# Leaf rows of two trees added on VectorE before the transpose, the low part of x on POOL, and one semaphore signal for each pair of halves

## The chip, the cores and the metric

The kernel runs on one core of a Trainium2 chip. The metric is the device time of one execution in microseconds (us). The program works through 32 units (pairs of images) in a software pipeline: three unrolled bodies fill it, a hardware loop runs over units 2 to 29, three unrolled bodies drain it.

## The reference, cut to what matters

```python
h = patchify(x) @ W.T + b                       # 64 images, 196 tokens, 768 -> 256
n = layernorm(h)
xn = n / max(norm(n) / 16, eps) * g
uv = silu(xn @ uv_w.T)                          # u (512), v (512), base (128)
q, k = rope(base * gamma + beta)
a = u * (square(relu((q @ k.T + w_rel) / sqrt(128))) @ v)
h = h + (n * res_scale + a @ o_w.T)
y = layernorm(h)                                # fast feed-forward: 8 trees of depth 7
logits = y @ W_in.T + b_in                      # 8 trees x 255 nodes
walk = root, then left or right by the sign of the node's logit, 7 times
out = h + (silu(logits) * on_the_walk) @ W_out.T
```

Only the 8 nodes on a token's walk through each tree contribute. In trees 0 to 3 the kernel treats the leaf apart: it fetches one row of a table in DRAM for each token (input weights, bias, output weights of the leaf that the walk ends in), forms the leaf's logit as a dot product, and adds `silu(logit) * output row`.

## The kernel before, in words

All large products run in float32 as three matmuls (`product`, lines 1140 to 1144): a value is split into a high part (rounded, made on ScalarE by `high`) and a low part (value minus high part, a subtraction on VectorE by `low`, line 835). A product is `hi*lo + lo*hi + hi*hi`. A unit has 392 tokens, held as 4 groups of 98.

One body of the pipeline works on up to four units at once: `p`, `i`, `n`, `nx` follow each other, `nx` is being loaded and embedded, `n` is in layer norm and attention, `i` and `p` are in the trees. Each engine has its own hand-written list of steps, `body(p, i, n, nx)`, and executes it in that order; semaphores tie the lists together. The steps that matter here:

- Embedding: ScalarE `x_high(n, k)`, VectorE `x_low(n, k)`, TensorE `embed(n, k)` for six chunks k in a ring of three buffers. `embed` signals `x_used` after every chunk.
- First layer norm: `turn_h(n, 0, m)` transposes h on TensorE in two halves m, VectorE `norm_stats` and `norm_moments`, POOL `norm_roots` (a power, a product, a product), ScalarE `norm_apply` and `make_xn`, TensorE `turn_xn` in two halves, ScalarE `xn_high`, VectorE `xn_low`, TensorE `turn_normed` in two halves, VectorE `residual(n, 0)` and `(n, 1)`, TensorE `make_base`, ScalarE `silu_base`, TensorE `make_v`. `make_base` waits for `residual(n, 0)`, since both use bank 0 of `front`; `make_v(n, 1)` writes that bank again and waits for `silu_base`.
- Trees: `tree_logits(i, t, b)` (b counts halves of 128 nodes), VectorE `decisions`, TensorE `tree_visits`, ScalarE `silu_tree`, VectorE `mask`, ScalarE `hid_high`, VectorE `hid_low`, TensorE `tree_out(i, t, m)` into `out_acc`, VectorE `final`, then the store.
- Leaves of trees s = 0 to 3: TensorE `find_leaf(i, s)`, ScalarE `leaf_number`, POOL `fetch_rows(i, s, g)` (one indirect DMA for each group g), VectorE `leaf_dots(i, s)`, ScalarE `leaf_silu` and `scale_rows(i, s)` (four products of 98x256), TensorE `add_rows(i, s)`: eight transposes that add the scaled rows into `out_acc` (line 1378). The rows lie in eight slots, so that two trees are held at a time; `fetch_rows(i, s, 0)` waits until `add_rows` of two trees before has freed the slots.

POOL otherwise makes the low parts of late weights (`split_late`, line 445), in the first two bodies only.

Of the kernel before, what the change touches and what calls it, by code (L numbers as in the profile page):

```python
# [24 lines left out]
ALU = mybir.AluOpType  # L25
# [19 lines left out]
DC = D // P  # L45
# [10 lines left out]
XRING = 3  # L56
UV = 2 * E + S
# [5 lines left out]
ROW_IN, ROW = D + 1, 2 * D + 1  # L63
ROW_SLOTS = 8
# [51 lines left out]
def vit_tower(nc, x, cols, tok_w, uv_w, o_w, in_w, out_w, rel, rope, anc, ident_in, out):  # L116
    ctx = ExitStack()
    with ctx:
# [121 lines left out]
        rows_added, held_ok = sem("rows_added"), sem("held_ok")  # L240
# [195 lines left out]
        def _(pool):  # L436
# [9 lines left out]

            def norm_roots(n, which):
# [13 lines left out]
            def fetch_rows(i, s, g):  # L461
# [3 lines left out]
                if g == 0:  # L465
# [3 lines left out]
                    if GROUPS * (s + 1) > ROW_SLOTS or not first(i):  # L469
                        pool.wait_ge(rows_added, GATHERED * i + s + 1 - ROW_SLOTS // GROUPS)  # L470
# [15 lines left out]
            def body(p, i, n, nx):  # L486
# [6 lines left out]
                fetch_rows(i, 1, 0)  # L493
                late_splits(i, n, 2)
                fetch_rows(i, 1, 1)
# [8 lines left out]
                late_splits(i, n, 4)  # L504
                fetch_rows(i, 3, 1)
                fetch_rows(i, 3, 2)
                fetch_rows(i, 3, 3)
                norm_roots(n, 1)
                norm_roots(nx, 0)
# [16 lines left out]
        def _(act):  # L526
# [3 lines left out]
            def x_high(n, k):  # L530
# [3 lines left out]
                if k >= XRING or not first(n):  # L534
                    act.wait_ge(x_used, n * XC + k - XRING + 1)
# [5 lines left out]
            def copy_h(n, m):  # L541
# [3 lines left out]
                if m == 0:  # L545
                    act.wait_ge(x_used, n * XC + XC)
# [48 lines left out]
            def scale_base(n, which):  # L595
# [3 lines left out]
                if which == 1:  # L599
                    act.wait_ge(normed_turned, 2 * n + 2)  # L600
# [47 lines left out]
            def ffn_x_high(n, m):  # L648
                if n is None:
                    return  # L650
                act.wait_ge(ffn_x_turned, 2 * n + m + 1)
                if m == 0 and not first(n):
                    act.wait_ge(logits_ready, HALVES * n)
# [12 lines left out]
            def silu_tree(i, t, b):  # L666
# [5 lines left out]
                if b == 1:  # L672
                    act.wait_ge(logits_ready, HALVES * i + halves_before(t + 1))
# [12 lines left out]
            def hid_high(i, t):  # L686
# [3 lines left out]
                if t >= 2 or not first(i):  # L690
                    act.wait_ge(tree_added, 2 * (TREES * i + t - 1))
# [38 lines left out]
            def body(p, i, n, nx):  # L730
                silu_tree(p, 7, 1)
# [3 lines left out]
                silu_tree(p, 7, 0)  # L735
                copy_h(n, 1)
                scale_rows(p, 3)
                hid_high(p, 7)
                silu_tree(i, 0, 0)
                hid_high(i, 0)  # L740
                silu_tree(i, 1, 0)
                norm_apply(n, 0, 0)
                norm_apply(n, 0, 1)
                norm_apply(n, 0, 2)
                leaf_number(i, 0)
                silu_tree(i, 2, 0)
# [4 lines left out]
                make_xn(n, 3)  # L751
                leaf_number(i, 1)
# [3 lines left out]
                leaf_number(i, 2)  # L756
                hid_high(i, 2)
                silu_tree(i, 3, 0)
                x_high(nx, 0)
                silu_base(n)  # L760
                scale_base(n, 1)
                scale_base(n, 0)
                leaf_silu(i, 0)
                silu_v(n, 0)
# [802 lines left out]
```

## Time and profile before

| | |
|---|---|
| median of 3 runs | 2202.95 us (2196.44 to 2209.55) |
| the profiled execution | 2201.36 us |
| its span, first to last instruction | 2199.5 us |
| TensorE matmul busy | 2066.1 us (94%) |
| VectorE busy | 1621.5 us (74%) |
| ScalarE busy | 1395.2 us (63%) |
| POOL busy | 774.1 us (35%) |

Busy times count an engine's own instructions. Matmuls overlap in the array and their ends are modelled, so 94% is not the share of what the array could do; the pitch from one start to the next is the better measure. Idle time of an engine costs something only where another waits for it, in the end TensorE.

### The profile page before, as it was taken

The page shows a single profiled execution, that of the slowest core. Times are in us where ns is not written, and L with a number is a line of the kernel's source. Part 1 is how long each engine was busy: PE and PEld are TensorE (multiplying, and loading weights), DVE is VectorE, ACT ScalarE, POOL GpSimd, SP SyncE. Part 2 cuts the span into 40 slices and gives each one's busy share as a digit, 9 for nine tenths or more (in the row PEclk, how much of TensorE's full clock was granted, in tenths as well). Part 3 has the DMA queues.
Part 4 walks back from the last instruction along what each step waited for, and adds up shares of the span by engine and source line. Part 5 has one row for each costly group of instructions (what it writes and reads, how often), then busy time and mean ns, then how long its engine had stood idle before and what let it go on. Part 6 is the DMA issues. An engine that isn't in the chain of part 4 may idle for free.

```text
span 2199.5 us, 42461 instructions
## 1 busy us (share of the span) xinstructions
PE 2066.1 (94%) x13256; PEld 1941.8 (88%) x13256; DVE 1621.5 (74%) x4210; ACT 1395.2 (63%) x3085; POOL 774.1 (35%) x905
## 2 busy tenths in 40 slices
PE   6899999999999999999999999999999999999997
PEld 5789889899988898888998898988889988889887
DVE  5678777777777787777777777777777877777775
ACT  5556666666666566566666665666665666656654
POOL 2752333232333333332323333323323233333233
PEclk8999999999999999999999999999999999999999
DMA  5331322222322223222223222222223232222222
GB/s 146 85 94 52 89 73 66 73 76 63 83 71 65 81 55 84 75 64 73 77 62 84 70 73 73 64 75 77 65 70 84 55 85 69 73 73 66 63 67 74
DMA packets 81999, 163.13 MB, mean 74 GB/s; under 512 B 17102, under 2 KB 48048, under 8 KB 81968
## 3 DMA queue, kind: packets, MB, share of 16 engines
q0 software_dynamic: 40960, 103.02, 17.4%
q1 hardware_dynamic: 41008, 59.71, 9.3%
q8 instruction: 17, 0.28, 0.1%
q14 instruction: 14, 0.11, 0.0%
HBM read 148.76 MB, written 13.90 MB: 74 GB/s over the span
## 4 chain that ended last, share of the span: by engine, by line
PE 84%; another core or an unknown queue 5%; ACT 4%; POOL 3%; issue 2%; DVE 1%; DMA 1%; ACTq 0%; POOLq 0%; SPq 0%; DVEq 0%
PE front L1142 10%; PE front L1144 9%; PE front L1143 9%; PE hid_ps L1142 9%; PE hid_ps L1143 9%; PE hid_ps L1144 9%; PE out_acc L1142 6%; PE out_acc L1143 6%; PE out_acc L1144 6%; PE out_acc L1378 4%; PE front L1177 2%; PE front L1184 2%; PE hid_ps L1366 2%; PE hid_ps L1337 2%
## 5 line engine op out<-in xcount | busy, mean ns | idle before, releaser
L474 POOL DMA_INDIRECT leaf_rows<-leaf_table,leaf_at x512 | 532.4, 1040 | 163.9 <-issue 163.4
L453 POOL TENSOR_TENSOR inv_root<-to_root,minus_half 98x8 f32<-98x8 f32 x64 | 111.0, 1734 | 728.3 <-DVE to_root L885 404.6
L528 ACT ACTIVATE hid_hi<-hid 128x392 fp32r<-128x392 f32 (+1 forms) x256 | 177.8, 695 | 237.1 <-PE out_acc L1144 155.4
L1142 PE MATMUL out_acc<-hid_hi,outw_lo 128*128 128x392 f32 x768 | 293.4, 382 | 2.6 <-DVE hid_lo L835 2.3
L1142 PE MATMUL hid_ps<-ffn_x,in_lo 128*128 128x392 f32 x768 | 282.3, 368 | 6.2 <-POOL in_lo L445 5.8
L1143 PE MATMUL hid_ps<-ffn_x,in_hi 128*128 128x392 f32 x768 | 266.3, 347 | 0.0
L1144 PE MATMUL hid_ps<-ffn_x,in_hi 128*128 128x392 f32 x768 | 264.7, 345 | 0.0
L1144 PE MATMUL out_acc<-hid_hi,outw_hi 128*128 128x392 f32 x768 | 264.6, 345 | 0.0
L1143 PE MATMUL out_acc<-hid_lo,outw_hi 128*128 128x392 f32 x768 | 264.4, 344 | 0.0
L473 POOL TENSOR_TENSOR held<-minus_half 98x1 f32<-98x1 f32 x128 | 47.2, 369 | 489.9 <-issue 428.7
L718 ACT ACTIVATE leaf_rows<-leaf_rows,leaf_act 98x256 f32<-98x256 f32 x512 | 218.2, 508 | 0.1
L996 DVE SCALAR_TENSOR_TENSOR hid<-hid_ps,hid 128x392 f32<-128x392 f32 x384 | 203.1, 557 | 11.7 <-PE hid_ps L1337 11.3
L835 DVE TENSOR_TENSOR hid_lo<-hid,hid_hi 128x392 fp32r<-128x392 f32 (+1 forms) x256 | 196.0, 766 | 13.8 <-ACT hid_hi L528 9.4
L1015 DVE CUSTOM_DVE_ANT_0 leaf_rows<-leaf_rows,leaf_x 98x257 f32<-98x257 f32 x512 | 188.2, 421 | 16.8 <-DMA leaf_rows<-leaf_table,leaf_at 16.4
L980 DVE TENSOR_SCALAR decide<-hid_ps,col 128x392 bf16<-128x392 f32 x256 | 156.4, 620 | 38.6 <-PE hid_ps L1144 35.5
L683 ACT ACTIVATE hid<-hid_ps,col 128x392 f32<-128x392 f32 x256 | 150.9, 590 | 38.1 <-DVE decide L980 38.1
L1142 PE MATMUL front<-uv_hi,xn 128*98 128x512 f32 x256 | 110.4, 431 | 51.1 <-ACT bases L593 43.3
L1142 PEld LDWEIGHTS hid_ps<-ffn_x,in_lo 128*128 128x128 f32 x768 | 149.6, 195 | 7.1 <-POOL in_lo L445 6.4
L1142 PE MATMUL front<-xn,uv_lo 128*128 128x392 f32 x320 | 113.9, 356 | 43.6 <-issue 42.2
L1142 PEld LDWEIGHTS out_acc<-hid_hi,outw_lo 128*128 128x128 f32 x768 | 147.2, 192 | 8.6 <-DVE hid_lo L835 3.0
L1143 PEld LDWEIGHTS out_acc<-hid_lo,outw_hi 128*128 128x128 f32 x768 | 147.6, 192 | 3.2
L1143 PEld LDWEIGHTS hid_ps<-ffn_x,in_hi 128*128 128x128 f32 x768 | 148.2, 193 | 0.0
(140 smaller groups left out, 5808.2 us busy)
## 6 DMA issues: line engine op xcount, KB each, us to landing
x_raw<-x SPq DMA_DIRECT2D x192, 196.0 KB, 2.4
out<-out_stage SPq DMA_DIRECT2D x32, 392.0 KB
leaf_rows<-leaf_table,leaf_at POOLq DMA_INDIRECT x512
leaf_table<-leaf_rows SPq DMA_DIRECT2D x4, 256.5 KB, 4.7
out_stage<-in_w SPq DMA_DIRECT2D x4, 256.0 KB
tok_major<-tok_w SPq DMA_DIRECT2D x3, 256.0 KB, 4.3
late_raw<-out_w SPq DMA_DIRECT2D x6, 128.0 KB
u<-uv_w SPq DMA_DIRECT2D x1, 576.0 KB, 4.2
```

Source lines behind the costliest of these rows:

```text
L453: pool.tensor_tensor(inv_root[:, 0:size], to_root[:, 0:size], minus_half[:, 0:size], ALU.pow).then_inc(roots_ok, 1)
L474: pool.indirect_dma_start(row_slot(s, g), None, table, bass.IndirectOffsetOnAxis(ap=leaf_at[:, s, g:g + 1], axis=0), element_offset=s * P ...
L528: act.activation(out, src, ACT.Copy).then_inc(done, 1)
L683: act.activation(hid_t[:, t % 2, b], hid_ps[:, t % 2, b, 0:T], ACT.Silu, bias=bias).then_inc(activated, 1)
L718: act.activation(w, w, ACT.Copy, scale=leaf_act[:, s, g:g + 1]).then_inc(rows_scaled, 1)
L835: dve.tensor_tensor(out, src, hi.bitcast(F32), ALU.subtract).then_inc(done, 1)
L980: dve.tensor_scalar(decide[:, t % 2], hid_ps[:, t % 2, 0, 0:T], c(COL_B_IN + 2 * t), 0.0, ALU.add, ALU.is_gt).then_inc(decided, 1)
L996: dve.scalar_tensor_tensor(hid_t[:, t % 2, b], hid_ps[:, t % 2, 1, 0:T], VISITED[b], hid_t[:, t % 2, b], ALU.is_ge, ALU.mult).then_inc(mas ...
L1015: dve.tensor_tensor_reduce(w, w, normed2[:, g], 1.0, 0.0, ALU.mult, ALU.add, leaf_logit[:, s, g:g + 1]).then_inc(dotted, 1)
L1142: pe.matmul(out, w[1], x_parts[0], start=start, stop=False)
L1143: pe.matmul(out, w[0], x_parts[1], start=False, stop=False)
L1144: return pe.matmul(out, w[0], x_parts[0], start=False, stop=stop)
```

## The change

1. Leaf rows. ScalarE scales the rows of trees 0 and 2 only. VectorE has a new step, `merge_rows(i, s)` for s = 1 and 3: `row(s) * leaf_act(s) + row(s - 1)`, four instructions. `add_rows` is called for s = 1 and 3 alone and turns the sum. The slots of trees 0 and 2 are free once the merge is done (`rows_merged`), those of 1 and 3 after `add_rows`.
2. The low part of x is made on POOL (`x_low`) from the second unit on, VectorE keeps it for the first (`first_x_low`).
3. One signal for a pair of halves: `x_used` after chunks 2 and 5 only, `h_turned`, `xn_turned`, `normed_turned`, `ffn_x_turned`, `tree_added` after the second half, `logits_ready` after a tree's last half. The waits follow.
4. The lists of TensorE, VectorE and ScalarE are written in another order, and the bodies of TensorE, VectorE and ScalarE are cut at another place (TensorE's now begins with `tree_out(p, 0, 0)`).

```diff
+X_SIGNALS = (2, 5)
+COUPLES = GATHERED // 2
 # POOL
+            def x_low(n, k):
+                if n is None or first(n):
+                    return
+                if k == 0 and isinstance(n, int) and n == 1:
+                    pool.wait_ge(x_lo_ok, XC)
+                pool.wait_ge(x_hi_ok, n * XC + k + 1)
+                pool.tensor_tensor(x_lo[:, k % XRING], x_raw[:, k % XRING], x_hi[:, k % XRING].bitcast(F32),
+                                   ALU.subtract).then_inc(x_lo_ok, 1)
...
-                        pool.wait_ge(rows_added, GATHERED * i + s + 1 - ROW_SLOTS // GROUPS)
+                        couple = COUPLES * i + (s // 2 + 1 - ROW_SLOTS // GROUPS // 2)
+                        if s % 2 == 0:
+                            pool.wait_ge(rows_merged, GROUPS * couple)
+                        else:
+                            pool.wait_ge(rows_added, couple)
 # ScalarE
-                    act.wait_ge(x_used, n * XC + k - XRING + 1)
+                    act.wait_ge(x_used, 2 * n + k // XRING)
...
-                act.wait_ge(xn_turned, 2 * n + m + 1)
+                act.wait_ge(xn_turned, n + 1)
 # VectorE
+            def merge_rows(i, s):
+
+                if i is None:
+                    return
+                dve.wait_ge(leaf_active, GATHERED * i + s + 1)
+                dve.wait_ge(rows_scaled, GROUPS * (COUPLES * i + s // 2 + 1))
+                for g in range(GROUPS):
+                    one, two = (row_slot(n, g)[:, ROW_IN:ROW] for n in (s - 1, s))
+                    dve.scalar_tensor_tensor(two, two, leaf_act[:, s, g:g + 1], one,
+                                             ALU.mult, ALU.add).then_inc(rows_merged, 1)
...
-                dve.wait_ge(normed_turned, 2 * n + m + 1)
+                dve.wait_ge(normed_turned, n + 1)
...
-                dve.wait_ge(logits_ready, HALVES * i + halves_before(t) + 1)
+                dve.wait_ge(logits_ready, TREES * i + t + 1)
 # TensorE
-                last.then_inc(x_used, 1)
+                if k in X_SIGNALS:
+                    last.then_inc(x_used, 1)
...
-                last.then_inc(done, 1)
+                if m == DC - 1:
+                    last.then_inc(done, 1)
...
-                last.then_inc(logits_ready, 1)
+                if b == halves(t) - 1:
+                    last.then_inc(logits_ready, 1)
...
-                last.then_inc(tree_added, 1)
+                if m == DC - 1:
+                    last.then_inc(tree_added, 1)
...
-                pe.wait_ge(rows_scaled, GROUPS * (GATHERED * i + s + 1))
+                pe.wait_ge(rows_merged, GROUPS * (COUPLES * i + s // 2 + 1))
```

Where instructions now stand. First TensorE in the loop, from the transposes of `xn` to the second product for v (`tok_major` holds the normalised rows, `front<-xn,uv_lo` begins `make_base`, `front<-uv_hi,xn` is `make_v`, `out_acc` is `tree_out`, `leaf_steps` is `find_leaf`, `toward` is `tree_visits`). Before:

```order
L1184 MATMUL front<-ident,tok_major 128x98 [waits xn_tm_ok]
...
L1366 MATMUL hid_ps<-leaf_steps,taken 98x1 [waits masked,taken_ok]
...
L1184 MATMUL front<-ident,tok_major 128x98 [waits xn_lo_ok]
L1184 MATMUL front<-ident,tok_major 128x98 x3
L1142 MATMUL out_acc<-hid_hi,outw_lo 128x392 [waits hid_lo_ok]
...
L1337 MATMUL hid_ps<-decide,toward 128x392 [waits leaf_at_ok,masked,decided]
L1142 MATMUL front<-xn,uv_lo 128x392 [waits res_added]
...
L1142 MATMUL hid_ps<-ffn_x,in_lo 128x392 [waits leaf_at_ok,masked]
...
L1142 MATMUL front<-uv_hi,xn 98x512 [waits res_added]
...
L1142 MATMUL front<-uv_hi,xn 98x512 [waits base_ok]
```

Now:

```order
L1218 MATMUL front<-ident,tok_major 128x98 [waits xn_tm_ok]
...
L1403 MATMUL hid_ps<-leaf_steps,taken 98x1 [waits masked,taken_ok]
...
L1515 COMPARE_AND_BRANCH
L1174 MATMUL out_acc<-hid_hi,outw_lo 128x392 [waits hid_lo_ok,out_ready]
...
L1218 MATMUL front<-ident,tok_major 128x98 [waits xn_lo_ok]
L1218 MATMUL front<-ident,tok_major 128x98 x3
...
L1174 MATMUL out_acc<-hid_hi,outw_lo 128x392 [waits hid_lo_ok]
...
L1174 MATMUL front<-xn,uv_lo 128x392 [waits res_added]
...
L1174 MATMUL front<-uv_hi,xn 98x512 [waits res_added]
L1175 MATMUL front<-uv_lo,xn 98x512
L1176 MATMUL front<-uv_hi,xn 98x512
...
L1174 MATMUL front<-uv_hi,xn 98x512 [waits base_ok]
```

Both halves of `turn_normed` now stand together, two pieces of `tree_out` (six matmuls) stand between them and `make_base`, and one more piece stands between the two products for v. `tree_visits(i, 3)` and `tree_logits(i, 4, 0)` have moved ahead of the first `turn_normed`, and the loop's branch lies in this stretch.

Next POOL in the loop, from the last fetches of a body to its end. Before:

```order
L473 TENSOR_TENSOR held<-minus_half 98x1 [waits held_ok,rows_added,leaf_at_ok]
L474 DMA leaf_rows<-leaf_table,leaf_at 98x513 x4
L453 TENSOR_TENSOR inv_root<-to_root,minus_half 98x4 [waits moments_ok]
L456 TENSOR_TENSOR shift<-moments,inv_root 98x4 [waits roots_ok]
L453 TENSOR_TENSOR inv_root<-to_root,minus_half 98x8 [waits moments_ok]
```

Now:

```order
L488 TENSOR_TENSOR held<-minus_half 98x1 [waits held_ok,rows_added,leaf_at_ok]
L489 DMA leaf_rows<-leaf_table,leaf_at 98x513
...
L455 TENSOR_TENSOR x_lo<-x_raw,x_hi 128x392 [waits x_hi_ok]
...
L489 DMA leaf_rows<-leaf_table,leaf_at 98x513 x3
...
L464 TENSOR_TENSOR inv_root<-to_root,minus_half 98x4 [waits moments_ok]
...
L467 TENSOR_TENSOR shift<-moments,inv_root 98x4 [waits roots_ok]
...
L464 TENSOR_TENSOR inv_root<-to_root,minus_half 98x8 [waits moments_ok]
```

Three `x_low` stand between the first and the second fetch of tree 3, three more between the roots of the second layer norm and those of the first.

## Rows read from the trace of the kernel before

**Rows 1.** The page, part 1: busy us, share of the span, instructions.

```profile
PE 2066.1 (94%) x13256; PEld 1941.8 (88%) x13256; DVE 1621.5 (74%) x4210; ACT 1395.2 (63%) x3085; POOL 774.1 (35%) x905
```

**Rows 2.** Waits: engine, line, what it waited for: us, times, longest us.

```profile
ACT bases L591 <- remote: 115.5, 28, 4.2
...
PE front L1142 <- issue: 48.2, 36, 3.0
PE front L1142 <- ACT bases L593: 43.3, 25, 2.2
```

**Rows 3.** Timeline of TensorE, one iteration: start, us, instruction, [idle before <- releaser].

```profile
1013.82 1.04 PE L1177 MATMUL front<-ident,hT 128*98 128x128 f32 x8
...
1025.81 0.84 PE L1184 MATMUL front<-ident,tok_major 98*128 98x98 f32 x8
...
1027.75 0.53 PE L1184 MATMUL front<-ident,tok_major 98*128 98x98 f32 x4
...
1028.68 0.50 PE L1184 MATMUL front<-ident,tok_major 98*128 98x98 f32 x4
...
1030.59 0.44 PE L1142 MATMUL front<-xn,uv_lo 128*128 128x392 f32 x1 [1.24 <-issue]
...
1031.59 0.34 PE L1144 MATMUL front<-xn,uv_hi 128*128 128x392 f32 x1
...
1036.58 0.61 PE L1142 MATMUL front<-uv_hi,xn 128*98 128x512 f32 x1 [2.15 <-ACT bases L593]
```

**Rows 4.** Timeline of VectorE in the same stretch.

```profile
1029.91 0.62 DVE L899 SCALAR_TENSOR_TENSOR hT<-front,col,hT 128x392 f32<-128x392 f32 x1 [1.83 <-PE front L1184]
1032.11 0.63 DVE L899 SCALAR_TENSOR_TENSOR hT<-front,col,hT 128x392 f32<-128x392 f32 x1 [1.57 <-remote]
```

**Rows 5.** Timeline of ScalarE in the same stretch.

```profile
1023.15 1.73 ACT L577 ACTIVATE tok_major<-tok_major,xn_scale 98x256 f32<-98x256 f32 x4
...
1035.00 0.49 ACT L591 ACTIVATE bases<-front 64x392 f32<-64x392 f32 x1 [4.16 <-remote]
```

**Rows 6.** Timeline of POOL in the same stretch.

```profile
1017.97 2.35 POOL L453 TENSOR_TENSOR inv_root<-to_root,minus_half 98x8 f32<-98x8 f32 x1 [12.49 <-DVE to_root L885]
...
1023.43 1.05 POOL L474 DMA_INDIRECT leaf_rows<-leaf_table,leaf_at  x1 [0.65 <-issue]
...
1032.84 0.97 POOL L474 DMA_INDIRECT leaf_rows<-leaf_table,leaf_at  x1 [0.30 <-issue]
```

**Rows 7.** The page, part 2: granted TensorE clock, in tenths, 40 slices.

```profile
PEclk8999999999999999999999999999999999999999
```

**Rows 8.** Span and mean granted clock of the core.

```profile
core 0: 2199.5 us, clock 0.981
```

**Rows 9.** Stretches of 1 us: busy share (instructions) by engine, clock, DMA, GB/s.

```profile
1037.00:1038.00 1.00, 1.00 (x4) 0.71 (x3) 0.04 (x1) 1.00 (x3) 0.00 (x0) 0.50 0.00 0
```

**Rows 10.** Timeline of TensorE: one call of `add_rows` and the matmuls behind it.

```profile
1044.76 0.84 PE L1378 MATMUL out_acc<-ident,leaf_rows 98*128 98x98 f32 x8
...
1045.64 0.34 PE L1143 MATMUL out_acc<-hid_lo,outw_hi 128*128 128x392 f32 x1
```

**Rows 11.** Groups of instructions: count, busy us, mean ns, idle before and releasers.

```profile
L1015 DVE CUSTOM_DVE_ANT_0 leaf_rows<-leaf_rows,leaf_x 98x257 f32<-98x257 f32 x512 | 188.2, 421 | 16.8 <-DMA leaf_rows<-leaf_table,leaf_at 16.4
...
L1378 PE MATMUL out_acc<-ident,leaf_rows 98*128 98x98 f32 x1024 | 107.3, 247 | 1.0 <-ACT leaf_rows L718 1.0
L835 DVE TENSOR_TENSOR x_lo<-x_raw,x_hi 128x392 fp32r<-128x392 f32 x192 | 106.2, 567 | 32.9 <-ACT x_hi L528 32.9
...
L835 DVE TENSOR_TENSOR v_lo<-v_full,v_hi 98x512 fp32r<-98x512 f32 x128 | 86.2, 694 | 20.8 <-ACT v_hi L528 20.8
...
L445 POOL TENSOR_TENSOR o_lo<-late_raw,o_hi 128x512 fp32r<-128x512 f32 x1 | 1.3, 1287 | 0.1
```

**Rows 12.** Timeline of VectorE near 96 us, while POOL makes a low part.

```profile
96.26 2.39 DVE L835 TENSOR_TENSOR v_lo<-v_full,v_hi 98x512 fp32r<-98x512 f32 x2
```

**Rows 13.** Timeline of POOL near 96 us.

```profile
95.99 1.50 POOL L445 TENSOR_TENSOR outw_lo<-late_raw,outw_hi 128x512 fp32r<-128x512 f32 x1
```

More of the change, by code:

```diff
@@ L835, in low, with first_x_low @@
                 dve.tensor_tensor(out, src, hi.bitcast(F32), ALU.subtract).then_inc(done, 1)
[L837 to L838 removed]
+            def first_x_low(n, k):
+                if n is None or not first(n):
                     return
[L840 removed]
+                dve.wait_ge(x_hi_ok, k + 1)
                 low(x_lo[:, k % XRING], x_raw[:, k % XRING], x_hi[:, k % XRING], x_lo_ok)
[L842 removed]
+                if k % 2 == 0:
                     dve.wait_ge(front_w_hi, k // 2 + 1)
@@ L1076, in body @@
                 v_low(n, 1)
+                first_x_low(nx, 4)
+                first_x_low(nx, 5)
+                mask(i, 4)
                 qk_low(n, 0)
+                leaf_dots(i, 1)
                 qk_low(n, 1)
-                leaf_dots(i, 1)
-                if first(n):
-                    build_toward()
-                hid_low(i, 3)
+                merge_rows(i, 1)
                 v_low(n, 2)
-                mask(i, 4)
                 add_rel_bias(n, 0)
@@ L1394, in body @@
             def body(p, i, n, nx):
+                tree_out(p, 0, 0)
+                turn_normed(i, 0)
+                turn_normed(i, 1)
+                tree_out(p, 0, 1)
+                tree_out(p, 1, 0)
+                make_base(i)
+                tree_logits(p, 4, 1)
+                make_v(i, 0)
+                tree_out(p, 1, 1)
+                make_v(i, 1)
+                find_leaf(p, 3)
+                tree_visits(p, 4)
+                tree_logits(p, 5, 0)
+                make_v(i, 2)
+                tree_out(p, 2, 0)
+                make_v(i, 3)
+                tree_logits(p, 5, 1)
                 make_u(i, 0)
                 make_u(i, 1)
-                tree_visits(p, 4)
-                tree_logits(p, 5, 1)
+                tree_logits(p, 6, 0)
                 scores(i, 0)
                 scores(i, 1)
+                add_rows(p, 1)
+                tree_logits(p, 6, 1)
+                make_u(i, 2)
+                tree_out(p, 2, 1)
                 tree_out(p, 3, 0)
-                make_u(i, 2)
                 make_u(i, 3)
-                tree_logits(p, 6, 0)
-                add_rows(p, 1)
                 mix(i, 0)
                 tree_visits(p, 5)
-                tree_logits(p, 6, 1)
                 mix(i, 1)
@@ L1417, in body @@
                 project_o(i, 1, range(0, EC))
-                embed(n, 0)
+                tree_out(p, 4, 1)
                 turn_h(i, 1, 0)
                 turn_h(i, 1, 1)
-                tree_out(p, 4, 1)
+                embed(n, 0)
                 embed(n, 1)
+                embed(n, 2)
                 tree_logits(p, 7, 0)
                 tree_logits(p, 7, 1)
-                embed(n, 2)
                 embed(n, 3)
                 embed(n, 4)
+                tree_visits(p, 7)
                 embed(n, 5)
-                add_rows(p, 2)
                 turn_ffn_x(i, 0)
```

171 lines of the change are left out of this document (78 added, 93 removed).

## The prediction

> **What bounds the kernel now.** I first read the busy shares [rows 1]: TensorE is at 94%, the next engine, VectorE, at 74%. So time leaves the kernel in three ways only: less work on TensorE, less idle time of TensorE, or a higher clock while it works. Next the waits of TensorE [rows 2]: it sat idle 48.2 us ahead of matmuls of line 1142 with no releaser told ("issue") and 43.3 us until the last `silu_base`. Together 91.5 us, nearly all of it in one stretch that comes once a unit, between the transposes of `xn` and the second product for v.
>
> The timeline of one iteration shows why. The first half of `turn_normed` is over at 1027.75 + 0.53 = 1028.28, the second at 1028.68 + 0.50 = 1029.18 [rows 3]. Yet the two `residual` instructions on VectorE that wait for them begin at 1029.91 and 1032.11 [rows 4], 1.6 and 2.9 us later, with VectorE idle. `make_base` waits for the first of them, which ends at 1030.53, and begins at 1030.59: this is the 1.24 us of "issue". Its last matmul ends at 1031.59 + 0.34 = 1031.93 [rows 3], but `silu_base` begins only at 1035.00 after 4.16 us of idle [rows 5], 3.1 us late. So the second product for v waits 2.15 us more [rows 3]. The waits of ScalarE show that this is the rule: 115.5 us in 28 waits of up to 4.2 us, as many as the loop has iterations [rows 2]. What is late is TensorE's own signals. They are late in just the time in which POOL issues eight row fetches in a row (first at 1023.43, last ending at 1033.81 [rows 6]), and later and later, like a queue that is served slowly. Counted in the code, TensorE gives ten signals from the last of `turn_xn` to that of `make_base`, in 6.1 us.
>
> These gaps also cost clock. Behind the second one the granted clock is 0.50, the lower of two levels, 1.2 instead of 2.4 GHz [rows 9]; the mean is 0.981 [rows 8], a loss of 0.019 x 2199.5 = 42 us. The first slice, at 0.8 [rows 7], is about 0.2 x 55 = 11 us of it, start-up; 31 us belong to the loop.
>
> **The change part by part.** The sum is made against the profiled execution's 2201.4 us, 1.6 below the median of 2202.95 and within the spread of the three runs; I add 1.6 at the end.
>
> *Half of the `add_rows` calls go.* 128 calls are 1024 transposes and 107.3 us busy [rows 11]; half is 53.7 us. The pitch says less: one call and the first matmul behind it take 1045.64 - 1044.76 = 0.88 us [rows 10]; a matmul alone takes 0.2 (five steps from 1030.59 to 1031.59 [rows 3]), so a call is 0.68 us and 64 calls are 44 us. It lies on TensorE, which has no cover. I take the pitch: **-44 us**, bounds 44 to 54.
>
> *`merge_rows`* are 8 instructions of 98x256 a unit on VectorE. The nearest row is `leaf_dots`, 98x257 with two inputs in SBUF, at 0.42 us [rows 11]: 3.4 us a unit. ScalarE loses 16 of 32 row products a unit. `x_low` takes six subtractions of 106.2/192 = 0.55 us off VectorE [rows 11], 3.3 us, so VectorE's load stays as it was.
>
> *`x_low` on POOL.* Rows of POOL give 1.29 us for the same operation on 512 columns [rows 11]; 392/512 of that is 0.99, so six take 6 us a unit of POOL, which is 65% idle. Queued behind the first three are the last three fetches of tree 3 and `norm_roots(n, 1)`, behind the other three `norm_roots(nx, 0)`. POOL has 12.49 us idle ahead of the latter [rows 6], so I cost the move at nothing there. It is tight in one place: `x_high(nx, 3)` now waits for chunk 2 (`x_used` is given twice), so 0.5 us on ScalarE and 1 us on POOL must fit under the two halves of `tree_logits(p, 7)` that stand before `embed(n, 3)`, about 2.1 us. It fits if POOL is free then; if not, TensorE waits. The two engines also hinder each other. Two `v_lo` took 2.39 us [rows 12] where 2 x 0.694 is 1.39 [rows 11], while POOL subtracted for 1.50 us [rows 13] instead of 1.29: VectorE lost 1.0 us, about 0.7 of POOL's time. With all six `x_low` over such work VectorE would lose 4 us a unit; that is the upper end, the lower is nothing.
>
> The Trainium skill, GPSIMD Engine Reference, Engine selection, speaks against this part: it wants two-input elementwise work on VectorE, POOL being about twice as slow, and its Key points say that POOL contends with VectorE instructions that read two inputs from SBUF. The trace agrees on both (1.0 against 0.55 us, and 1.0 us lost). By its ratio a subtraction would take 1.1 us instead of 0.99, which moves nothing in the sum.
>
> *The stalls at the base.* From the last of `turn_xn` to that of `make_base` the new code gives six signals (`turn_xn`, `tree_visits`, `find_leaf`, `turn_normed`, one of `tree_out`, `make_base`) in about 5 us, not ten in 6. Ahead of `make_base` there are now six matmuls of `tree_out`, some 1.1 us, to cover the signal and the first `residual` (0.62 us [rows 4]); ahead of the second product for v there is half a microsecond more. ScalarE reads the leaf numbers after `make_xn` now, so the fetches start nearer to `make_base` and less of the burst lies before it. If signals are late by under about half a microsecond at the first place, both waits are gone. The whole 91.5 us is the upper end; I take 80%: **-73 us**. The lower end is half, if the signals stay a microsecond late.
>
> *The clock.* Shorter gaps, fewer falls: of the 31 us I take 70%, **-22 us**; bounds 0 and 31.
>
> *New tight places.* The order leaves less room on the first norm's chain. Before, `turn_h` ends at 1013.82 + 1.04 = 1014.86 and `turn_xn` begins at 1025.81 [rows 3], while `make_xn` was done at 1023.15 + 1.73 = 1024.88 [rows 5]: 0.9 us of room. TensorE's list now has one block of six matmuls (1.1 us) less between these two, and the chain is shortened by a few tenths only (`norm_moments` and `norm_apply` no longer wait behind other steps). `tree_visits(i, 2)`, just ahead, now waits for a leaf number behind `make_xn`. I expect 0 to 1.5 us a unit and take 0.5 over 31 units: **+15 us**, bounds 0 and 46. In the start-up six `x_low` stand behind late weights on POOL: **+3 us**, bounds 0 and 6.
>
> Sum: -44 - 73 - 22 + 15 + 3 = -121; 2201.4 - 121 + 1.6 = **2082 us**. With every term at its good end 2201.4 - 54 - 91 - 31 + 1.6 = 2027, at its bad end 2201.4 - 44 - 46 - 0 + 46 + 6 + 1.6 = 2165.
>
> **Rivals.**
> *The signals stay late.* If not their number but the row fetches delay them, the base stalls remain and only the transposes are saved: 2201.4 - 44 + 15 + 3 + 1.6, about 2177 us. For it: the lateness lies within the fetches. Against it: the lateness grows from signal to signal, 1.6, 2.9, 3.1 us, and the new order gives both waits more cover anyhow. The Trainium skill, TensorE: Matmul & The Clock Gate, The cost: per-tile semaphore tail, would side with it: signals serialise at 26.3 ns each, so four fewer save 0.1 us. The 1.6 to 3.1 us seen here are far from that, so no such price explains the rows, and I give the case a low chance.
>
> *A merge wait takes the place of the old one.* `add_rows(p, 3)` stands just behind `turn_h(n, 0)`, at the start of a stretch without room, and now needs `leaf_dots`, `leaf_silu` and `merge_rows` one after the other. Before, it waited 1.0 us in the whole run [rows 11]. If it comes 2 us late in 31 units, that is +62, and half of the clock gain goes: 2082 + 62 + 11, about 2155 us.
>
> *POOL holds up VectorE (slower).* Place: from `embed(n, 3)` to `turn_xn`, where `x_low` 3 to 5 run beside `leaf_dots`, `merge_rows` and `hid_low`, all with two inputs in SBUF. VectorE would lose 3 x 0.7 us and TensorE wait a further microsecond for `x_low(3)`: 3.1 us a unit, +96 over 31 units. With the base stalls kept and more falls of the clock (+20), 2177 + 96 + 20 is about 2293 us. It makes the kernel slower once its price passes 44 - 18 = 26 us, 0.8 us a unit, while the stalls stay; if they go, only above 3.9 us a unit. For it: rows 12 and 13. Against it: VectorE is idle 26% of the time, and the last three `x_low` leave VectorE in just this stretch.
>
> *The change may not do what it says*, if `add_rows` waited as long as it saved; that is the merge rival with 1.5 us a unit.
>
> **How the numbers follow.** Chances: 66% for the forecast (own range 2027 to 2165), 14% for late signals (2177), 11% for the merge wait (2155), 9% for POOL holding up VectorE. The range from 2035 to 2185 takes in the first three nearly whole and leaves out the last and the best end. About 0.5%, 11 us, is what a measurement of this kernel can tell from no change, so faster means below 2192. The first three cases lie there but for a margin: faster 0.87, within 0.5% 0.05, slower 0.08.
>
> **What would show it.** Right: `add_rows` 512 transposes and about 53 us busy; in the waits of TensorE the entries for `bases` and "issue" well below 91.5 us; `silu_base` waiting less than 115.5 us; a mean clock above 0.981. Wrong: TensorE waiting for `leaf_rows`, `x_lo` or `tok_major`, or `v_lo`, `hid_lo` and the merges well above 0.42 to 0.7 us while POOL subtracts. The forecast falls if `residual` still begins microseconds after `turn_normed`.

## The result, and the profile after

The changed kernel takes 2327.88 us (median of 4 runs, 2307.49 to 2333.47) beside 2203.7 us (2196.44 to 2209.55) for the kernel before: a ratio of 1.0548, 95% interval 1.0477 to 1.062. The prediction, 2082 us with a range from 2035 to 2185, was wrong in sign. The profiled execution took 2329.88 us, span 2328.1 against 2199.5, mean granted clock 0.943 against 0.981 [rows 8].

The first part of the page after, which answers to [rows 1]:

```profile
PE 2111.1 (91%) x12744; PEld 1973.6 (85%) x12744; DVE 1732.4 (74%) x4280; ACT 1309.4 (56%) x2829; POOL 934.4 (40%) x1091
```

512 instructions of TensorE are gone, yet its busy time rose by 45 us: what is left ran at a lower clock. The waits of TensorE and of ScalarE after (engine, line, what it waited for: us in total, times, longest), beside [rows 2]:

```profile
PE front L1174 <- ACT bases L614: 75.7, 28, 3.8
PE front L1174 <- DVE u L966: 56.6, 29, 2.0
PE front L1174 <- issue: 18.5, 32, 2.4
...
ACT bases L612 <- remote: 115.8, 30, 5.5
```

The two entries at the base are 75.7 + 18.5 = 94.2 us where they were 91.5, and `silu_base` waits 115.8 us where it waited 115.5: nothing was won there. And there is an entry that the kernel before did not have: 56.6 us for `u`, which line 966, `gate`, writes. Two groups of instructions after, beside [rows 11] (count, busy us, mean ns, idle before and releasers):

```profile
L1034 DVE CUSTOM_DVE_ANT_0 leaf_rows<-leaf_rows,leaf_x 98x257 f32<-98x257 f32 x512 | 277.0, 594 | 15.7 <-DMA leaf_rows<-leaf_table,leaf_at 13.4 <-issue 2.1
...
L1415 PE MATMUL out_acc<-ident,leaf_rows 98*128 98x98 f32 x512 | 54.8, 251 | 0.1
```

`add_rows` is halved and waits for nothing, as forecast. The leaf dots, untouched by the change, went from 421 to 594 ns.

**The account.** Added over the trace, the gaps of TensorE longer than 0.15 us, without the wait for its first matmul, are 122.0 us before and 204.8 us after: +82.8. The clock costs (1 - 0.981) x 2199.5 = 41.8 us before and (1 - 0.943) x 2328.1 = 132.7 after: +90.9. Together that is 173.7 us, while the spans differ by 128.6: 45.1 us are left over for work that is gone, beside the 44 us forecast for the transposes. By the place of the records at half clock, about 53 us of the 133 follow the gap at the base and 61 us the new one.

**The new gap.** The timeline of one iteration after, all engines, cut to the rows that matter (start, us, instruction, [idle before <- releaser]):

```profile
1052.55 0.57 DVE L966 SCALAR_TENSOR_TENSOR u<-front,u 128x392 f32<-128x392 f32 x1 [0.69 <-issue]
1053.03 3.39 DVE L1034 CUSTOM_DVE_ANT_0 leaf_rows<-leaf_rows,leaf_x 98x257 f32<-98x257 f32 x1
...
1053.11 3.02 POOL L455 TENSOR_TENSOR x_lo<-x_raw,x_hi 128x392 fp32r<-128x392 f32 x3
...
1055.74 0.34 PE L1176 MATMUL out_acc<-hid_hi,outw_hi 128*128 128x392 f32 x1
...
1056.35 0.43 DVE L1034 CUSTOM_DVE_ANT_0 leaf_rows<-leaf_rows,leaf_x 98x257 f32<-98x257 f32 x1
...
1057.41 1.03 DVE L966 SCALAR_TENSOR_TENSOR u<-front,u 128x392 f32<-128x392 f32 x2
...
1058.02 0.36 PE L1174 MATMUL front<-kern_parts,v_lo 98*128 98x196 f32 x1 [1.94 <-DVE u L966]
```

The first of `leaf_dots(i, 2)` takes 3.39 us, its three neighbours 0.41 to 0.43; its end, 1056.42, falls just behind the end of POOL's three subtractions at 1056.13. `gate(n, 1)`, next on VectorE, starts 3 us late at 1057.41, and `mix(i, 3)`, whose bank that gate must free, leaves TensorE idle for 1.94 us. It comes in 29 iterations. (The expectations below call this product `mix(i, 2)`; counted along the timeline it is the fourth, `mix(i, 3)`.)

**The old gap.** The same iteration, earlier:

```profile
1022.13 1.05 POOL L489 DMA_INDIRECT leaf_rows<-leaf_table,leaf_at  x1 [0.64 <-issue]
...
1026.48 1.16 DVE L918 SCALAR_TENSOR_TENSOR hT<-front,col,hT 128x392 f32<-128x392 f32 x2 [1.69 <-PE front L1218]
...
1028.16 0.34 PE L1176 MATMUL front<-xn,uv_hi 128*128 128x392 f32 x1
...
1031.25 0.97 POOL L489 DMA_INDIRECT leaf_rows<-leaf_table,leaf_at  x1 [0.30 <-issue]
...
1032.28 0.49 ACT L612 ACTIVATE bases<-front 64x392 f32<-64x392 f32 x1 [4.06 <-remote]
...
1033.86 0.47 PE L1174 MATMUL front<-uv_hi,xn 128*98 128x512 f32 x1 [2.38 <-ACT bases L614]
```

`make_base` ends at 1028.50; `silu_base` begins at 1032.28, 3.8 us later and 0.06 us behind the last of the eight fetches (1031.25 + 0.97). Before it was 3.1 us [rows 3, 5]. `residual` is less late now (0.9 us behind `turn_normed`, not 1.6 to 2.9); that part of the wait moved on to the second product for v.

One stretch of 1 us behind the new gap of another iteration (busy share and instructions by engine, then TensorE's clock, the DMA share and GB/s) shows what such a gap brings:

```profile
771.00:772.00 1.00, 1.00 (x5) 1.00 (x6) 1.00 (x3) 0.85 (x2) 0.70 (x2) 0.50 0.72 254
```

0.50 is the lower of the two levels, 1.2 GHz, as in [rows 9]; TensorE had been idle until 770.86.

### The profile page after: what moved, and what is told of

The parts are those of the page before. It is cut to its first block, busy times and chain, and to the rows that moved or that the text cites. A ratio compares the mean times of both kernels' runs of the same rounds, so it can differ in the third digit from the quotient of the medians.

```text
span 2328.1 us, 41334 instructions
## 1 busy us (share of the span) xinstructions
PE 2111.1 (91%) x12744; PEld 1973.6 (85%) x12744; DVE 1732.4 (74%) x4280; ACT 1309.4 (56%) x2829; POOL 934.4 (40%) x1091
## 4 chain that ended last, share of the span: by engine, by line
PE 63%; DVE 18%; another core or an unknown queue 7%; issue 6%; ACT 3%; POOL 2%; DMA 0%; DVEq 0%; ACTq 0%; SPq 0%; POOLq 0%
PE hid_ps L1174 7%; PE hid_ps L1175 7%; PE hid_ps L1176 7%; PE front L1174 7%; PE front L1175 6%; PE front L1176 6%; DVE leaf_rows L1034 6%; PE out_acc L1174 5%; PE out_acc L1176 5%; PE out_acc L1175 5%; PE front L1210 2%; DVE hid_lo L854 2%; PE front L1218 2%; DVE decide L999 1%
## 5 line engine op out<-in xcount | busy, mean ns | idle before, releaser
L489 POOL DMA_INDIRECT leaf_rows<-leaf_table,leaf_at x512 | 542.6, 1060 | 150.4 <-issue 148.5
L464 POOL TENSOR_TENSOR inv_root<-to_root,minus_half 98x8 f32<-98x8 f32 x64 | 91.9, 1436 | 629.8 <-DVE to_root L894 340.6
L1174 PE MATMUL hid_ps<-ffn_x,in_lo 128*128 128x392 f32 x768 | 291.6, 380 | 8.4 <-POOL in_lo L447 8.4
L1034 DVE CUSTOM_DVE_ANT_0 leaf_rows<-leaf_rows,leaf_x 98x257 f32<-98x257 f32 x512 | 277.0, 594 | 15.7 <-DMA leaf_rows<-leaf_table,leaf_at 13.4
L1175 PE MATMUL out_acc<-hid_lo,outw_hi 128*128 128x392 f32 x768 | 270.8, 353 | 0.0
L1176 PE MATMUL out_acc<-hid_hi,outw_hi 128*128 128x392 f32 x768 | 270.5, 352 | 0.0
L1174 PE MATMUL front<-kern_parts,v_lo 98*128 98x196 f32 x512 | 155.1, 303 | 58.0 <-DVE u L966 56.6
L455 POOL TENSOR_TENSOR x_lo<-x_raw,x_hi 128x392 fp32r<-128x392 f32 x186 | 188.8, 1041 | 3.5 <-ACT x_hi L549 2.5
L1174 PE MATMUL front<-uv_hi,xn 128*98 128x512 f32 x256 | 112.9, 441 | 82.1 <-ACT bases L614 75.7
L549 ACT ACTIVATE xn<-u 128x392 fp32r<-128x392 f32 x128 | 66.8, 536 | 173.7 <-DVE u L966 166.8
L1174 PEld LDWEIGHTS front<-kern_parts,v_lo 98*128 98x128 f32 x512 | 106.3, 208 | 68.4 <-DVE u L966 66.6
```

The lines of the kernel that those rows point to most:

```text
L455: pool.tensor_tensor(x_lo[:, k % XRING], x_raw[:, k % XRING], x_hi[:, k % XRING].bitcast(F32), ALU.subtract).then_inc(x_lo_ok, 1)
L464: pool.tensor_tensor(inv_root[:, 0:size], to_root[:, 0:size], minus_half[:, 0:size], ALU.pow).then_inc(roots_ok, 1)
L489: pool.indirect_dma_start(row_slot(s, g), None, table, bass.IndirectOffsetOnAxis(ap=leaf_at[:, s, g:g + 1], axis=0), element_offset=s * P ...
L549: act.activation(out, src, ACT.Copy).then_inc(done, 1)
L1034: dve.tensor_tensor_reduce(w, w, normed2[:, g], 1.0, 0.0, ALU.mult, ALU.add, leaf_logit[:, s, g:g + 1]).then_inc(dotted, 1)
L1174: pe.matmul(out, w[1], x_parts[0], start=start, stop=False)
```

## Experiments

Two theories. **A**: a VectorE instruction that reads two operands from SBUF stands still while POOL subtracts beside it. **B**: TensorE's signals are late because POOL issues a row of fetches at that time. Against B stands **C**, the step of the prediction: they are late because there are many of them. Ratios are to the kernel before on the same chip. In the expectations v0 to v3 and u are the products `make_v(n, 0)` to `(n, 3)` and `make_u`, so "the gap before v1" is the wait ahead of the second product for v.

### Moving POOL's low parts (A)

```diff
-                x_low(nx, 0); x_low(nx, 1); x_low(nx, 2)
                 fetch_rows(i, 3, 1); fetch_rows(i, 3, 2); fetch_rows(i, 3, 3)
+                x_low(nx, 0); x_low(nx, 1); x_low(nx, 2)
```

> The changed kernel with one move in POOL's list: the low parts 0 to 2 of x stand behind the last three row fetches of the unit instead of ahead of them. Theory A (the custom leaf dot stands still while POOL's subtractions run beside it): the first dot of tree 2 is back from 3.39 to about 0.42 us, the wait of mix(i, 2), 56.6 us over 29 units, goes, and with it most of the 63 us of clock lost right behind it: 2328 - 57 - (40 to 63) = 2208 to 2231 us. Rival (the dot is long for another reason, such as the row fetch just ahead of it): the dot stays above 3 us and the time within 15 us of 2328.

Measured: 2337.01 us, ratio 1.0581 (1.0546 to 1.0616). The time is the rival's, but not for its reason. The timeline, all engines:

```profile
1059.81 3.00 POOL L455 TENSOR_TENSOR x_lo<-x_raw,x_hi 128x392 fp32r<-128x392 f32 x3
1059.82 4.37 DVE L854 TENSOR_TENSOR qk<-u,xn 128x392 fp32r<-128x392 f32 x3
...
1064.34 0.67 PE L1174 MATMUL front<-xn,o_lo 128*128 128x392 f32 x1 [2.97 <-DVE qk L854]
```

(The move also joins the fetches of trees 2 and 3 into a row of eight; no new wait of TensorE for it shows.) The leaf dots are back at 426 ns on average, and what now starts together with POOL, the three `mix_low`, takes 4.37 us instead of 1.51. `project_o` waits for them, 87.0 us over 30 iterations. The block moved with POOL's work, so A stands; the time I wrote down for it failed because I had not looked at what would stand in the new place.

### Holding half of the fetches (B against C)

```diff
+                if n is not None:
+                    pool.wait_ge(base_ok, n + 1)
                 fetch_rows(i, 1, 0)
```

> The changed kernel with one wait added on POOL: the four row fetches of tree 1 start only when silu_base of the unit has ended, so that four and not eight fetches stand in a row ahead of it. Theory B (TensorE's signals arrive late while POOL works through a row of fetches): silu_base begins within 1 us of make_base's end instead of 3.8 us behind it, the gap of TensorE before v1 (79 us over 30 units) falls by 60 to 79 us and the clock lost there (51 us) by 30 to 51: 2198 to 2238 us; what lateness is left shows at v2, v3 and u. Rival C (lateness comes from the number of TensorE's signals, the fetches only happen to run then): the gap stays above 60 us and the time within 15 us of 2328, or above it by what leaf_dots(i, 1) now waits.

> The kernel before with the one wait on POOL alone: the row fetches of tree 1 start behind silu_base. Theory B: the stalls at the bases (93 us over the units) fall by 60 to 90 us, and of the 43 us of clock loss the 24 behind them go for the most part: 2095 to 2130 us. Rival C: within 15 us of 2204, or above it by what leaf_dots(i, 1) waits for its rows.

Measured: the changed kernel falls from 2327.88 to 2202.91 us (ratio 0.9984, 0.9968 to 0.9999), the kernel before from 2207.77 to 2107.58 us (ratio 0.9548, 0.952 to 0.9576), both inside what B expects. Of the entries in [rows 2] the one for `bases` is gone in both. What TensorE waits for then, the kernel before with the held fetches:

```profile
PE front L1144 <- DVE hT L901: 17.9, 30, 0.7
PE hid_ps L1144 <- POOL in_lo L445: 10.5, 2, 8.2
```

and the changed one with them:

```profile
PE front L1176 <- DVE u L968: 57.1, 30, 2.1
PE front L1176 <- issue: 13.0, 27, 0.5
```

From the semaphore events of the trace, the signal of `make_base` is 3.77 us late on average in the changed kernel, 0.02 with the fetches held, 2.60 in the kernel before and 0.05 there with them held. The signals are the same in each pair, so their number alone cannot be the cause. The clock follows: 0.990 in the kernel before with held fetches.

What the hold removes is the coincidence. With it `make_base` ends 0.7 us or more after the last fetch of the row of four, in every iteration of the loop in both kernels. `turn_normed` of the changed kernel still ends within that row, and its signal is as late as before: 0.91 us on average with the hold, 0.84 without.

### What in the fetches holds the signals

The two runs change the length of the row, and the bytes of a fetch.

```diff
 fetch_rows(i, 1, 2)
+                if n is not None:
+                    pool.wait_ge(base_ok, n + 1)
+                    ... (a 98x1 multiplication that carries the wait)
 fetch_rows(i, 1, 3)
```

> The changed kernel with only the last of the eight row fetches held back until silu_base has ended (a tiny POOL instruction carries the wait), so that seven and not eight or four stand in a row ahead of it. Theory B (a signal of TensorE that falls into the row of fetches is held until the row ends): the row ends one fetch, 1.28 us, earlier, so silu_base begins 2.4 to 2.6 us behind make_base's end (3.76 with eight, 0.4 or less with four), the gap before v1 is 1.2 to 1.5 us instead of 2.63, 35 to 43 us less over 30 units, and 2241 to 2295 us come out, the more the clock follows. Rival C (number of signals): gap of 2.4 us or more and a time within 15 us of 2328.

```diff
-table: 513 columns; row_slot(s, g) <- table
+table: 257 columns; row_slot(s, g)[:, 0:257] <- table
```

> The changed kernel with the leaf table cut to the first 257 of its 513 columns, so that each of the 512 row fetches moves half the bytes with as many rows and instructions; what the rows would add to the output is left out of the fetch (the second half of each slot keeps old contents, worked on as before). Theory B, by instructions (what holds the signals is the number of fetches, not their bytes): silu_base stays 3 us or more behind make_base's end, the gap before v1 stays within 15 us of 79 and the time within 25 us of 2328. Theory B, by bytes: delay and gap fall by half, 35 to 45 us and part of the 51 us of clock, 2235 to 2295 us.

Measured with seven: 2307.96 us (2278.81 to 2332.84, too scattered for a ratio), a gap of 2.07 us against 2.63 and 62.1 us for `bases`. The direction is B's, but half its size: `make_base`'s signal is still 3.23 us late on average. It does not simply wait for the row's end. With half the bytes: 2314.73 us, ratio 1.0455 (1.0428 to 1.0482), and

```profile
PE front L1175 <- ACT bases L615: 68.1, 30, 3.0
PE front L1175 <- DVE u L967: 56.7, 29, 2.0
```

`make_base`'s signal is 3.42 us late (3.77 with full rows). That is what theory B by instructions expects: the bytes matter little.

What matters is how far the row has come. Sorted by the number of fetches begun when the matmul ended, the signals within the rows of eight were, in the changed kernel, 0.01 us late (median) in the first and second fetch, 0.9 in the third, 1.8 in the fourth, 3.8 in the fifth and 4.1 in the sixth; in the kernel before 0.01, 0.01, 0.3, 1.3 and 2.9 in the first five. (A few semaphore events are missing from the traces, so single pairs can be wrong.) `make_base` of the changed kernel ends in the fifth.

### The number of signals

Three runs: the old signals in the changed kernel, the new ones in the kernel before, without and with held fetches.

```diff
-                if m == DC - 1:
-                    last.then_inc(done, 1)
+                last.then_inc(done, 1)        # and likewise for logits, tree_out, turn_h, embed
```

In the two runs of the kernel before the same lines go the other way.

> The changed kernel with the two signals for each pair of halves put back and nothing else. Theory B: as the fetches stay eight in a row, the gap before v1 stays within 15 us of 79 and the time within 20 us of 2328. Rival C, the step of the forecast: with nearly twice the signals of those parts the gap grows by half or more, 40 us and its clock: 2370 us or more.

> The kernel before with one part of the change alone: one signal for each pair of halves (transposes, embed, logits, tree_out), everything else and all orders as before. Rival C, which is the step of the forecast: the stalls at the bases, 93 us before, fall by about 73 and the clock loss by 22: near 2108 us. Theory B: the stalls stay within 20 us of 93 and the time within 15 us of 2204.

> The kernel before with the fetches of tree 1 held behind silu_base and with one signal for each pair of halves, so both parts that were run apart (2107.6 and 2452.8 us) together. Theory D (a single signal is held long only inside the long row of fetches): the wait for residual ahead of make_base, 190 us with the row of eight, is below 40 us, and with it most of the 245 us that the single signals cost: 2105 to 2150 us. Rival (in the old order the single signals cost that much anyway, since each waits for the later half): 2300 us or more.

All three missed what I wrote. With two signals the changed kernel is faster, 2283.66 us, ratio 1.0379 (1.0362 to 1.0396): the wait for `bases` falls, another for `v_full` comes up behind it:

```profile
PE front L1173 <- ACT v_full L634: 34.1, 30, 1.5
...
PE front L1173 <- ACT bases L613: 21.4, 14, 3.7
```

The single signals alone make the kernel before slower by 11%: 2452.77 us, ratio 1.1118 (1.1086 to 1.115). Its timeline, all engines:

```profile
1065.20 0.50 PE L1187 MATMUL front<-ident,tok_major 98*128 98x98 f32 x4
...
1069.40 0.97 POOL L475 DMA_INDIRECT leaf_rows<-leaf_table,leaf_at  x1 [0.30 <-issue]
...
1071.78 1.16 DVE L900 SCALAR_TENSOR_TENSOR hT<-front,col,hT 128x392 f32<-128x392 f32 x2 [7.13 <-remote]
...
1072.46 0.70 PE L1143 MATMUL front<-xn,uv_lo 128*128 128x392 f32 x1 [6.59 <-DVE hT L900]
```

The one signal of `turn_normed` is due at 1065.70 and comes at 1071.76, 1.4 us behind the end of the last fetch. So C is not just absent, its sign is wrong here: over the rows of eight fetches the late signals are about 1.9 us late on average with two signals a pair, in the old order and in the new, and about 2.8 us (new order) and 3.5 us (old order) with one. These averages are over different signals; for one and the same place, `silu_base` begins 2.26 us behind the end of `make_base` with two signals in the new order and 4.04 us with one, on average over the loop.

With held fetches and single signals the kernel before takes 2279.05 us, ratio 1.0335 (1.0302 to 1.0368): 174 us less than without the hold, but still 171 more than with two signals. The wait for `residual` did fall, from 168.6 to 29.1 us; the rest is another cost:

```profile
PE hid_ps L1145 <- DVE x_lo L838: 59.6, 62, 1.3
PE front L1145 <- DVE hT L902: 29.1, 31, 1.0
PE front L1145 <- DVE u L950: 25.5, 32, 2.2
```

`embed` waits for low parts that cannot be made before the chunk buffers are given back in threes, and so on: in the old order each reader now waits for the later half. The new order has room for that: once both holes are closed, single signals cost next to nothing in it, as the last run below shows.

### Low parts alone, and both holes closed

The kernel before with its low parts on POOL, in the places of the change:

```diff
 VectorE:  -  x_low(nx, 0) ... x_low(nx, 5)        (from the second unit on)
 POOL:        fetch_rows(i, 3, 0)
           +  x_low(nx, 0); x_low(nx, 1); x_low(nx, 2)
              ...
              norm_roots(n, 1)
           +  x_low(nx, 3); x_low(nx, 4); x_low(nx, 5)
```

> The kernel before with one part of the change alone: the low parts of x on POOL, 0 to 2 behind the first fetch of tree 3 and 3 to 5 behind the second norm's root, as in the change. Theory A: about 3 us of POOL's run fall on the leaf dots of tree 2 or on mix_low behind them, one of them is longer by 2.5 to 3.0 us a unit, mix(i, 2) or project_o waits 1.5 to 2.5 us, 45 to 75 us over the units and 20 to 60 of clock: 2265 to 2335 us. The forecast's price (0 to 4 us a unit on VectorE, hidden): within 15 us of 2203.

Measured: 2223.1 us, ratio 1.0054 (1.0017 to 1.0092). The block is there, but smaller than I wrote:

```profile
999.53 2.58 DVE L1030 CUSTOM_DVE_ANT_0 leaf_rows<-leaf_rows,leaf_x 98x257 f32<-98x257 f32 x1
...
999.78 2.04 POOL L453 TENSOR_TENSOR x_lo<-x_raw,x_hi 128x392 fp32r<-128x392 f32 x2
...
1003.69 0.36 PE L1157 MATMUL front<-kern_parts,v_lo 98*128 98x196 f32 x1 [0.58 <-DVE u L962]
```

Only two low parts are ready together in the old order, 1.0 us less of POOL, and the old order has six matmuls of `tree_logits(p, 6)` between `mix(i, 0)` and `mix(i, 3)` where the new one has three of `tree_out(p, 3)`, half a microsecond more room. 1.94 less 1.5 is near the 0.58 us seen here; the wait is 18.6 us in all. The 56.6 us are thus the price of the move in the new order; that the order without the move does not have this gap is shown below, with the low parts back on VectorE.

Then the changed kernel with held fetches, and the low parts 0 to 2 once held until the last `mix_low`, once back on VectorE, and the first of these with two signals again:

```diff
                 fetch_rows(i, 3, 3)
+                if n is not None and nx is not None:
+                    pool.wait_ge(mix_lo_ok, EC * (n + 1))
                 x_low(nx, 0)
```

```diff
 VectorE:     mask(i, 6)
           +  x_low(nx, 0)
              update_h(n, 0)
           +  x_low(nx, 1)
              update_h(n, 1)
           +  x_low(nx, 2)
              ...
              leaf_dots(p, 3)
           +  x_low(n, 3); x_low(n, 4)
              decisions(p, 7)
           +  x_low(n, 5)
 POOL:     -  x_low(nx, 0) ... x_low(nx, 5)
```

> The changed kernel with the fetches of tree 1 held behind silu_base, and POOL's low parts 0 to 2 of x held until VectorE has ended the fourth mix_low, so that they run beside mask and update_h, which read one operand from PSUM. Theory A (only VectorE instructions with two operands in SBUF stand still while POOL subtracts): nothing is blocked, the gap before mix(i, 2) or project_o (57 us) goes, the 56 us of clock lost behind it too for the most part: 2090 to 2115 us. Rival (any VectorE instruction stands still then): mask or update_h takes 3 us more, turn_h of the unit is late by 1.5 to 2.5 us, and 2140 to 2175 us come out.

> The changed kernel with the fetches of tree 1 held behind silu_base and all low parts of x back on VectorE (0 to 2 around update_h, 3 to 5 behind the last leaf dots), so that the orders, the merged rows and the single signals are left of the change. Theory A: the gap before mix(i, 2) (57 us) and the clock lost behind it (56 us) go: 2090 to 2110 us, up to 2135 if the 2.9 us more per unit on VectorE delay update_h or the second norm by up to 1 us. Rival (the gap before mix(i, 2) belongs to the new order of VectorE's list and not to POOL): the gap stays, 2190 us or more.

> The kernel of the run before that holds both the fetches of tree 1 and the low parts 0 to 2 (2077 us), with the two signals for each pair of halves put back. Theory D (fewer signals are each held longer, but only within a long row of fetches): without the row of eight the number matters little, 2067 to 2087 us. The forecast's step (more signals are delivered later): 2095 us or more. Fewer signals harm everywhere: 2060 us or less.

Measured: 2077.21 us (ratio 0.9442, 0.9426 to 0.9458), 2077.67 us (0.9433, 0.9418 to 0.9449) and 2073.14 us (0.937, 0.935 to 0.9391). The first two end below what I expected; 13 and 12 us under it. The timeline of the first, all engines, decides on the other part of A:

```profile
1010.08 1.98 DVE L1019 SCALAR_TENSOR_TENSOR hid<-hid_ps,hid 128x392 f32<-128x392 f32 x4
...
1010.33 3.04 POOL L455 TENSOR_TENSOR x_lo<-x_raw,x_hi 128x392 fp32r<-128x392 f32 x3 [3.25 <-DVE qk L858]
...
1011.97 0.56 DVE L985 TENSOR_TENSOR h_kept<-front,hT 128x392 f32<-128x392 f32 x1
```

Beside the same three subtractions four `mask` take 1.98 us, as they do in the changed kernel, where no subtraction runs beside them, and `update_h` 0.56: they read one operand from PSUM and are not held up. The gap before `mix(i, 3)` is gone in both runs, the clock is 0.992 and 0.990. From the changed kernel with the hold alone (2202.91 us) that is 125 us less: 57 of gap, and a clock loss of 17 instead of 75 us. The third, run on another chip, shows that with the row ahead of `silu_base` broken up the number of signals weighs little, under 1% in the ratio and 4 us in the time.

Two things follow that the forecast did not ask for. The second run, with all low parts on VectorE, is as fast as the first, so the move to POOL gains nothing even where it harms nothing. And the kernel before with the one wait takes 2107.58 us: beside it merged rows and new orders are worth some 30 us, not 125 (ratios of 0.9548 and 0.9442). The merged rows were not run without the new orders. All three kernels still have a row of eight fetches in each iteration (those of trees 2 and 3), and signals that fall into its sixth fetch are 2.3 to 3.5 us late by the median; no wait of TensorE that recurs with the iterations is over 0.7 us there. A long row costs time only where something waits for its late signals.

## Why the prediction was wrong, point by point

- **What bounds the kernel** held: idle time and clock of TensorE, with the forecast's 44 us for the transposes, make 129.7 us where the spans differ by 128.6.
- **Half of `add_rows`, -44**: about right. Busy time fell by 107.3 - 54.8 = 52.5 us, and the account leaves 45.1. The same account between the two kernels without either hole (spans of 2108.9 and 2074.0 us) leaves about 37, so it is good to some 8 us.
- **`merge_rows`** mostly took 0.47 to 0.49 us each, a little over the 0.42 forecast, and one in each iteration 0.99 us, beside a subtraction of POOL. TensorE's wait at `add_rows` is 0.1 us in the whole run: the rival of 2155 us did not come.
- **`x_low` on POOL, "I cost the move at nothing there"**: this step failed. The rows were right, the reading was not. `v_lo` ran from 96.26, POOL to 95.99 + 1.50 = 97.49 [rows 12, 13]; I turned the 1.0 us lost into a share, "about 0.7 of POOL's time", and a load to be spread over a quarter of idle VectorE. It is a standstill: of the 1.23 us that POOL still ran beside it, VectorE lost 1.0, so three subtractions in a row make 3 us at one place, whatever the mean load. The prediction's slower rival, given 9% and left out of the range, had this mechanism, but at `embed(n, 3)` to `turn_xn`, where TensorE waited 3.0 us for `x_lo` in the whole run; with the base stalls unchanged it came to 2293 us. The place was behind `gate(n, 0)`: 56.6 us, and about 61 of clock. The Trainium skill, SBUF — State Buffer, SBUF: two separate sides, says that the port pair of VectorE and POOL is an exclusive lock, not a split of bandwidth, taken for a whole instruction, also against VectorE instructions with two operands in SBUF. The runs agree: 3.39 us for a 0.42-us dot, 4.37 for 1.51, and nothing lost beside reads of PSUM. The section also has the one that starts first win; as far as the records tell that is not so here, since the dot of the run with the low parts alone began at 999.53, POOL at 999.78, and the dot was held.
- **The stalls at the base, -73**: this step failed altogether; its two entries went from 91.5 to 94.2 us. I argued that six signals instead of ten would be served sooner. With the fetches held, the signal of `make_base` is 0.01 to 0.05 us late with single signals and with two alike, and within the row fewer signals came later. The argument held against the rival "signals stay late", that lateness grows from signal to signal, fits a row of fetches just as well, in which lateness grows with the place in the row. That rival had the cause right; its 2177 us left out the low parts. The cover of half a microsecond ahead of the second product for v was eaten by 0.7 us more lateness in the iteration shown.
- **The clock, -22**: +91. That the clock follows the gaps was right; the gaps were not shorter. Where both are closed the loss is 0.008 x 2074.0 = 17 us, 25 less than before, so the size was fair for stalls that go.
- **New tight places, +15**: the first norm's chain cost nothing in the loop. A gap of 0.26 us at the loop's branch, which now lies in this stretch and which no term priced, adds 7.3 us in 27 iterations; at its old place there was none. The start-up cost about 8 us, not 3: two gaps before `turn_xn` went from 5.2 to 8.5 us together, one before `tree_logits` from 3.5 to 8.4.

The sum of 2082 us is close to what the changed kernel takes once both holes are closed (2077 us), but that is no point for the forecast: the base stalls went there by a wait that the change does not have. It missed that the change's own new placement adds a gap, and that the row of fetches, which the change leaves in place, keeps the old one.

What stays open: which rule lets a signal through inside the row. In several iterations, late signals of the kernel before came one by one, some 0.7 us apart, while the row lasted and close together after it; in the changed kernel mostly 0.7 or 1.4 us apart, and where there were more signals each came sooner. The runs show that, not why.

## What to carry to other kernels

Before work goes to POOL, look at which VectorE instructions will run beside it: next to POOL's two-operand subtractions, those with two operands in SBUF stopped until POOL was done, those with one in PSUM did not, and the price was paid at that place and not in the mean load. Where signals of TensorE are late, look for a long row of indirect fetches on POOL at the same time and move the later ones away with one wait, before anything is done about the signals: one wait brought the untouched kernel from 2208 to 2108 us. A signal left out makes its reader wait for the later half, so it needs an order that has room for that.

## What the runs showed of the hardware

- Signals of TensorE came 0.01 us after their instruction nearly everywhere, and up to 6.2 us after it (`turn_normed` with one signal) within a row of eight indirect fetches, from the third fetch on. The Trainium skill, TensorE: Matmul & The Clock Gate, The cost: per-tile semaphore tail, gives 26.3 ns for each signal of a row of tile matmuls and says that one on the last tile is safe and saves the others' time; beside such a row of fetches the measured lateness is some seventy times that, and one signal was the slower choice (about 2.8 against 1.9 us).
- Halving the bytes of a fetch left the lateness of `make_base` at 3.42 us (3.77); with the row ended before it, it was 0.02.
- The VectorE instruction that is held stands still through three POOL subtractions back to back, 3.0 us, although they are separate instructions.
- A gap of 2 us cost about as much again in clock: 56.6 us of gaps before `mix(i, 3)`, some 61 us lost at the lower level behind them; with the fetches held, closing these gaps took the loss from 75 to 17 us.
